# Adding an attention mask on VectorE, head by head, instead of on TensorE

## The reference, cut to what matters

```
scores = jnp.einsum('btkgd,bskd->bkgts', qg, k) * scale       # layer 0
mask = jnp.tril(jnp.ones((T, T), dtype=scores.dtype))
scores = scores + mask[None, None, None]                      # +1, not -inf
p = jax.nn.softmax(scores, axis=-1)
...
scores = jnp.einsum('bhqd,bhkd->bhqk', qh, kh) * inv_sqrt_d   # layer 1
scores = jnp.where(causal, scores, jnp.finfo(scores.dtype).min)
attn = jax.nn.softmax(scores, axis=-1)
```

## Time and profile before

| | |
|---|---|
| median of three runs | 2088.39 us |
| the profiled execution, its own time | 2087.5 us |
| its span, first to last instruction | 2085.7 us |
| busy: TensorE (PE) | 1887.3 us, 90% |
| busy: VectorE (DVE) | 1041.1 us, 50% |
| busy: ScalarE (ACT) | 713.2 us, 34% |
| busy: GpSimd (POOL) | 385.6 us, 18% |
| mean granted TensorE clock | 0.967 |
| mask products L858, both phases | 2 x 19.1 us busy, 2 x 64 |
| maxima L715, both phases | 39.0 and 39.1 us busy, 2 x 32, mean 1.22 us |

### The profile page before, as it was taken

How to read it: one execution, slowest core, us unless ns; L and a number is a source line. 1 busy time by engine, 2 the same in 40 slices (tenths; PEclk the granted TensorE clock), 3 DMA queues, 4 the chain that set the end, 5 groups by cost and what they waited for, 6 DMA issues and landing times. The chain is left out here.

```text
span 2085.7 us, 32789 instructions
## 1 busy us (share of the span) xinstructions
PE 1887.3 (90%) x12124; PEld 1535.6 (74%) x12124; DVE 1041.1 (50%) x1836; ACT 713.2 (34%) x2275; POOL 385.6 (18%) x339
## 2 busy tenths in 40 slices
PE   8899888999999989999899998899879995999991
PEld 6667566788888767777677776677658874899990
DVE  5666753455555446333364547677865332222224
ACT  3555624334444332111231102545632210233332
POOL 1111100000000038000021100001104322745335
PEclk9999999999999999999999999999999998999995
DMA  7110142000000022000093000000015100644257
GB/s 238 42 46 14 43 160 82 1 1 1 1 1 1 1 76 91 1 0 0 24 352 115 1 20 27 26 2 1 2 46 207 46 0 0 243 149 143 82 114 205
DMA packets 73375, 135.89 MB, mean 65 GB/s; under 512 B 13456, under 2 KB 31760, under 8 KB 71184
## 3 DMA queue, kind: packets, MB, share of 16 engines
q1 hardware_dynamic: 47376, 96.28, 13.3%
q0 software_dynamic: 7888, 27.94, 4.5%
q10 hardware_dynamic: 17968, 9.71, 1.8%
HBM read 90.62 MB, written 43.29 MB: 64 GB/s over the span
## 5 line engine op out<-in xcount | busy, mean ns | idle before, releaser
L1473 PE MATMUL banks<-ternary_xth,ternary_wq 128*128 (+1 forms) x352 | 140.6, 399 | 5.0 <-DVE ternary_wq L1404 3.6
L1473 PE MATMUL banks<-ternary_xtl,ternary_wq 128*128 (+1 forms) x352 | 139.4, 396 | 0.0
L97 PE MATMUL banks<-latent_vh,latent_cth 128*128 128x512 f32 x256 | 104.2, 407 | 3.5 <-DVE latent_ctl L1174 3.5
L97 PE MATMUL banks<-weights,expert_xgh 128*128 x312 | 104.7, 336 | 2.4 <-DVE expert_xgl L2086 2.4
L99 PE MATMUL banks<-weights,expert_xgl 128*128 x312 | 101.6, 326 | 0.0
L573 ACT ACTIVATE gqa_pr<-banks,gqa_nb 128x128 f32<-128x128 f32 x256 | 90.4, 390 | 32.6 <-DVE gqa_nb L715 32.6
L98 PE MATMUL banks<-weights,expert_xgh 128*128 x312 | 101.4, 325 | 0.0
L573 ACT ACTIVATE causal_pr<-banks,causal_nb 128x128 f32<-128x128 f32 x256 | 90.4, 395 | 31.1 <-DVE causal_nb L715 31.1
L99 PE MATMUL banks<-latent_vh,latent_ctl 128*128 128x512 f32 x256 | 100.1, 391 | 0.0
L98 PE MATMUL banks<-latent_vl,latent_cth 128*128 128x512 f32 x256 | 100.1, 391 | 0.0
L1433 DVE TENSOR_TENSOR ternary_hf<-ternary_sg,banks 128x512 f32<-128x512 f32 x44 | 30.2, 687 | 135.4 <-issue 79.5
(11 more groups left out here) (462 smaller groups left out, 5412.0 us busy)
## 6 DMA issues: line engine op xcount, KB each, us to landing
x_slots<-decay_zeros SPq DMA_DIRECT2D x39, 256.0 KB, 4.3
y_slots<-decay_zeros SPq DMA_DIRECT2D x39, 256.0 KB, 4.5
y_slots<-expert_ys SPq DMA_DIRECT2D x39, 256.0 KB
expert_xin<-x_slots SPq DMA_DIRECT2D x38, 256.0 KB, 2.9
weights_raw<-in_expert_experts SPq DMA_DIRECT2D x4, 2176.0 KB, 9.2
gqa_tw<-in_ternary_w ACTq DMA_DIRECT2D x4, 2112.0 KB
ternary_raw<-in_ternary_w SPq DMA_DIRECT2D x11, 768.0 KB, 4.1
expert_raw<-in_expert_experts POOLq DMA_DIRECT2D x3, 2176.0 KB, 9.7
```

The costliest lines, as they stand in the source:

```text
L97: pe.matmul(out, wh, xh, start=first, stop=False, **kw)
L1473: a = pe.matmul(dst[:, :], wq[:, j, m, c * P:(c + 1) * P], x[:, c, toks], start=c == 0 and n == 0, stop=c == C - 1 and n == 1)
```

## The change

VectorE now adds the mask itself. For each of the 8 heads of a half there is one instruction on the 128x128 scores: it reads the head's scores from PSUM and the mask, writes -(scores + mask) back in place and folds the minimum of that into an accumulator, whose read is a second instruction. ScalarE's exponential takes the scores with a factor -1. ScalarE waits for the maxima twice per half, after four heads and after eight, instead of once. The four mask products per row are gone, as are the rounded copies of mask and identity at the start of a phase.

```diff
@@ -257,7 +257,7 @@
-            maskr, identr = sb("maskr", [P, P], F32R), sb("identr", [P, P], F32R)
+            mask = S.tril if kind == "gqa" else S.causal
@@ -564,14 +557,15 @@
                                    bias=bqk[:, 4 + h:5 + h]).then_inc(free_a, 1)
                 elif what == "S" and soft:
                     u = 2 * b + h
-                    act.wait_ge(max_done, u + 1)
                     if u >= 2:
                         act.wait_ge(pt_full, u - 1)
                     elif kind == "gqa":
                         act.wait_ge(ws_lo, 2)
                     for c in range(8):
+                        if c % 4 == 0:
+                            act.wait_ge(max_done, 2 * u + c // 4 + 1)
                         a = act.activation(pr[:, h, c, :], S.bank[2 * h + c // 4][:, (c % 4) * P:(c % 4 + 1) * P], ACT.Exp,
-                                           bias=nb[:, h, c:c + 1], accum_out=sums[:, b % 2, 8 * h + c:8 * h + c + 1])
+                                           scale=-1.0, bias=nb[:, h, c:c + 1], accum_out=sums[:, b % 2, 8 * h + c:8 * h + c + 1])
                     a.then_inc(exp_done, 1)
                 elif what == "mag":
                     if h == 0:
@@ -712,7 +706,14 @@
                     a.then_inc(free_d, 1)
                 elif what == "S" and soft:
                     dve.wait_ge(s_full, b + 1)
-                    dve.tensor_reduce(nb[:, h, :], unit_banks(h), AX, ALU.max, negate=True).then_inc(max_done, 1)
+                    if kind == "gqa" and u == 0:
+                        dve.wait_ge(S.loaded, 16 * len(S.tables))
+                    for c in range(8):
+                        s = S.bank[2 * h + c // 4][:, (c % 4) * P:(c % 4 + 1) * P]
+                        a = dve.tensor_tensor_reduce(out=s, in0=s, in1=mask[:, :], scale=-1.0, scalar=3e38,
+                                                     op0=ALU.add, op1=ALU.min, accum_out=nb[:, h, c:c + 1])
+                        if c % 4 == 3:
+                            a.then_inc(max_done, 1)
                 elif what == "S":
                     dve.wait_ge(s_full, b + 1)
                     dve.tensor_tensor(pt[:, b % 2, 8 * h:8 * h + 8, :], unit_banks(h), dec[:, 8 * h:8 * h + 8, :],
@@ -846,27 +847,19 @@
                 elif what == "S":
                     if h == 1:
                         continue
-                    if u == 0 and soft:
-                        pe.wait_ge(const_hi, 2)
                     if u % 8 == 0 and not (kind == "causal" and b == 0):
                         wait_freed(pe, ("q", b // GT, C - 1))
                         wait_freed(pe, ("k", b // GT, nk - 1))
                     if b >= 1:
                         pe.wait_ge(exp_done if soft else pt_done, u)
-                    if soft:
-                        for r in range(4):
-                            pe.matmul(S.bank[r], identr[:, :], maskr[:, :].unsqueeze(1).broadcast_to((P, 4, P)),
-                                      start=True, stop=False)
                     for j in range(4):
                         for r in range(4):
                             rows = slice(D * r, D * r + D)
                             q = qt[rows, b // GT % 2, j, tokens(b)]
                             k = kt[rows, b // GT % 2, j if nk > 1 else 0, tokens(b)]
                             dst = S.bank[r][:, j * P:(j + 1) * P]
-                            if soft:
-                                m = pe.matmul(dst, q, k, start=False, stop=j == 3)
-                            else:
-                                m = pe.matmul(dst, k, q, start=True, stop=True)
+                            lhs, rhs = (q, k) if soft else (k, q)
+                            m = pe.matmul(dst, lhs, rhs, start=True, stop=True)
                     m.then_inc(s_full, 1)
                 elif what == "T":
                     pe.wait_ge(exp_done, u + 1)
```

More of the change, by code:

```diff
@@ L532, in ternary_quarter @@
                 act.dma_start(tw[:, :, :, :], S.ternary[:, :, :, g * P:(g + 1) * P]).then_inc(tw_in, 16)
-            if kind == "causal":
-                constants()
             for e in act_plan:
```

## The result

The changed kernel takes 2092.31 us, the median of 15 runs (2083.22 to 2095.62). The kernel before, run beside it 15 times, takes 2085.77 us (2081.33 to 2089.57). The ratio is 1.003, with a 95% interval of 1.0021 to 1.004: slower by about 6 us, where 20.6 us had been forecast. The profiled executions have spans of 2092.9 and 2085.7 us, 7.2 us apart.

A forecast was written before the change was run, and what follows sets the result against it. VectorE's chain and TensorE were taken to bound each row in turn. 48.4 us for VectorE's maxima, less 33.6 for mask products, plus 5.8 for the clock gave +20.6 on 2087.5: 2108 us, range 2082 to 2160.

The forecast's parts named there:

- What bounds the kernel: Each attention row: VectorE sets the time from the end of the scores to rt, TensorE from rt to the scores.
- D: VectorE's added time per half, eight per-head maxima instead of one reduction: 1.10 us, bounds 0.54 to 2.38.
- Mask products: TensorE's four mask products before the scores, wholly on the path: 1.12 us saved in 30 rows, 33.6 us.
- Together 0.28 us for a head: VectorE's cost per head: 0.21 us for the 128x128 instruction and 0.07 for the accumulator read.
- 44 places: Times D delays TensorE over both phases, 0 to 3 per row by kind of row: 48.4 us added.
- The point of decision: D at which added and saved time balance: 33.6 / 44 = 0.76 us, 0.24 us per head on VectorE.
- 3 D: First two causal rows, said to hang on VectorE nearly throughout: three times D charged for them.
- Clock, 5.8 us: TensorE's clock falling behind longer waits before out in eight slotless rows: 5.8 us lost, half of the 11.5 bound.
- the free read: Rival: accumulator read hidden behind VectorE's next head, 0.21 us per head, -9.8 us, 2078 us; chance 0.10.
- no overlap: Rival: VectorE's instruction and read don't overlap, 0.44 us per head, +83.8 us, 2171 us; chance 0.19.
- TensorE as the bound: Rival: TensorE bounds the kernel and VectorE hides all its added work, -33.6 us, 2054 us; chance 0.01.
- Rival 2: Later waits absorb more: seven x or v rows carry 1 D, clock stays up, +7.1 us, 2095 us; chance 0.22.

The follow-up runs named there:

- the kernel with the larger D: Against the kernel before, VectorE adds the mask over 1024 columns in one instruction, then takes the maxima by the old reduction: 2135.06 us, ratio 1.0241.

## Why the prediction was wrong, step by step

The sign was right (slower), 2092.3 lies in the range, and the waits through which the change works are shown. The forecast change, 20.6 us, was three times too large.

1. *What bounds the kernel: right.* TensorE's waits before out and at rt have grown by D, in the rows that the working named: 1.02 to 1.84 us, 0.57 to 1.39 us.
2. *Mask products, 1.12 us in each row: right for most.* The kernel without mask has grouped q rows shorter by 1.12 us and slotless rows by 1.05, but rows 3 and 7 of the grouped phase are no shorter than the same rows with mask products in another execution. No gap came between pv and the scores.
3. *D, the term that was mis-sized.* The step "Together 0.28 us for a head" failed: it is 0.244. The 0.21 us of the instruction were good (0.20 measured), but to the read I had given the 0.07 us of a 128x1 instruction in the earlier trace rows, and with the accumulator it costs 0.045. D is 0.81 instead of 1.10 us. Over 44 places this is 44 x 0.29 = 12.8 us too much, where the forecast change missed by 14 us in all; the other errors, below, nearly cancel. By the prediction's own sum, 44 x 0.81 - 33.6 = +2.0 us. The point of decision, D = 0.76 us, was close to what came: 0.24 us per head against 0.244. At such a distance the sign hung on less than a hundredth of a microsecond per head, and that it came out right is luck. The rule of the Trainium skill that I had weighed ("VectorE: DVE Perf Modes", section "The DRAIN you can't avoid") doesn't show here in the starts: they stand 0.25 us apart at a duration of 0.33. The section says itself that an operation that isn't held starts earlier and sends the reader to the other one, "Two Vector instructions with no wait between them"; I had left that out. That one agrees with the rows: the read starts together with the next head.
4. *44 places: nearly.* The kinds with 1 D, 2 D and 0 D came out as said, except in the grouped x rows 4 and 8, whose first D costs 1.22 us, one addition of GpSimd, instead of 0.81: 0.8 us in all that the sum did not have. In the first two causal rows 3 D were too few. TensorE's waits there were 1.74 and 3.76 us before, and are 3.04, 1.11 and 5.40 us after, 4.05 us more, which is 5 D. The rows came out 2.77 us longer, but with the causal phase untouched they take 29.44 us in one kernel where before has 27.90, so that the size is uncertain by 1.5 us. Row 0 of the grouped phase came out 0.52 us longer, as 2 D would give where I had let waits take them; that isn't shown, since with the grouped phase untouched it takes 10.24 us too.
5. *Clock, 5.8 us: right as a mechanism, wrong in place and size.* I had expected it in the eight slotless rows. In the causal phase it is there in rows 12 to 14, at 0.3 to 0.45 us a row beyond the 2 D, since VectorE's chain lies over most of it; in the grouped phase the slotless rows show none in this execution, and up to 0.3 us a row with the grouped phase changed alone. Row 8 lost 0.2 us to it, and row 7 won 1.5 us back, which did not come again. Net this is about nothing, where 5.8 us had been forecast. The step behind the term was that the clock stays up behind a wait of 2.30 us. The trace of before has falls behind shorter waits, 2.28 us in row 3 (0.70 from 89 to 93 us) and 2.25 in row 7 (0.57), so that one wait could not tell when the clock stays up.

By these rows the sum stands so: +2.0 us by the 44 places with the D that was measured, 0.8 us for the two x rows, 2.6 for the first two causal rows (their 2.77 us against the 0.19 of 3 D), and a clock that gave about as much as it took; that is 5.4 us, against 6 to 7 between the medians. The terms are read from the two traces that they are to explain, and each of the last three is uncertain by a microsecond or more, so the agreement tests little.

Rivals: the free read (D = 0.54) is excluded by 0.244 us per head, though the value lies halfway between it and the forecast; no overlap (D = 2.38) and TensorE as the bound are excluded by the same rows and by the waits. Rival 2 gave nearly the time that came (2095), but by a mechanism that is not there: the causal rows with x or v do carry their 2 D.

## What to carry to other kernels

Where two engines take turns in setting a row, work moved from one to the other is charged by the number of places at which it reaches a wait, and not by busy time: here 1.12 us saved per row stood against 0, 1 or 2 times 0.81 us added, and the best version was the one that moved the work only in rows with 0 or 1. When such a sum is a small difference of large terms, the smallest instruction in the repeated pattern has to be measured, or the range has to lie on both sides of zero. A wait taken away by a new order has to be followed to the end of the row, through all that stands behind what was moved, on the other engines too. And before a difference of a few microseconds is split among stretches of two traces, the same stretches have to be read in kernels that leave them alone: here rows in the middle of a phase repeated to 0.1 us, but a whole phase only to 2 us.

## What the runs showed of the hardware

- The read of VectorE's accumulator starts together with the next instruction of the same engine: 128x128 folds are 0.22 to 0.25 us apart, 1.95 us for eight, at durations of 0.33 and 0.14 us. Plain instructions on the same tiles, read from PSUM and written back in place, are 0.20 us apart.
- An addition over 1024 columns of PSUM in place with a mask repeated eight times starts the reduction that waits for it 1.32 us later (1505.06 to 1506.38).
- VectorE's 128x512 remainder, 0.68 us long in the slotless rows, lasted 1.28 us beside two additions of GpSimd on the same shapes when it started within the first, and 1.68 us when it started within the second; in the first case GpSimd's second addition lasted 1.72 instead of 1.26 us.
- The granted clock fell behind waits of TensorE of 1.84 us (to 0.67), 2.25 (0.57), 2.27 (0.66), 2.47 (0.87, then 0.71) and 3.84 us (0.72 around it). The length of the wait alone doesn't tell it, since the same lengths stand on both sides: two waits of 1.39 and 1.36 us with 0.66 behind them in row 3 of the changed kernel and 1.00 in row 7, 2.05 and 2.06 us with 0.66 and 1.00 in the kernel with the larger D, and 2.30 us with 1.00 in the earlier trace rows where the same wait in the changed kernel, 2.29 us at 261.76, has 0.50 from 261 to 264 us. In the slotless row b=12 of the grouped phase of the changed kernel the wait before out is 1.83 us, and the clock stays at 1.00:

```profile
214.04 0.47 PE L97 MATMUL banks<-gqa_woh,gqa_oth 128*128 128x512 f32 x1 [1.83 <-DVE gqa_otl L740]
...
213.00:217.00 4.00, 2.96 (x12) 2.17 (x12) 4.00 (x23) 4.00 (x25) 0.00 (x0) 1.00 1.07 255
```

- Stretches of the program in which at most one row of the attention differs took 1051.9 to 1059.0 us and 574.0 to 584.3 us in single executions of eleven kernels. With other values in the scores they took 1051.4 and 573.7 us (no mask) and 1050.5 and 571.8 us (the plain instruction), just below that: whether the values had a part in it is not settled.
